# Selective scan at the end of a fused kernel: two replications issued ahead of the restacking, y sums, low part and x's turning moved within the step

## What is computed

```python
xs = stack([x0, x1, x0[..., ::-1], x1[..., ::-1]])     # 4 directions k: rows, columns, both reversed
x_dbl = einsum('bkdl,kcd->bkcl', xs, x_proj_weight)    # -> dts (6), Bs (16), Cs (16)
delta = softplus(einsum('bkrl,kdr->bkdl', dts, dt_projs_weight) + bias)
def step(h, inp):                                      # along the 4096 pixels
    h = exp(d_t[..., None] * A) * h + (d_t * u_t)[..., None] * B_t[:, :, None, :]
    y = einsum('bkdn,bkn->bkd', h, C_t)                # 96 channels x 16 states
ys = ys + Ds * xs; the four directions are turned back and summed; then a norm over channels
```

## Time and profile before

| what | value |
|---|---|
| 3 runs | 5444.3, 5447.71, 5461.19 us; median 5447.71 |
| profiled execution | 5458.66 us, span 5456.5 us |
| busy in the span | PE 4633.9 (85%), DVE 4354.1 (80%), POOL 4137.1 (76%), ACT 3138.7 (58%) |
| first and last scan | start 2764.0 us, end 5366.3 us: 2602.3 us for 128 steps |

### The profile page before, as it was taken

One profiled execution on the slowest core, in us unless ns is written; L12 is line 12 of the kernel. 1 busy time (PEld: TensorE's weight loads), 2 busy tenths in 40 slices (PEclk: granted clock), 3 DMA queues, 4 the chain that ended last, 5 costly groups with the idle time before them and its releaser, 6 DMA issues. The chain is left out here.

```text
span 5456.5 us, 68516 instructions
## 1 busy us (share of the span) xinstructions
PE 4633.9 (85%) x15210; PEld 2099.0 (38%) x15210; DVE 4354.1 (80%) x3524; ACT 3138.7 (58%) x6582; POOL 4137.1 (76%) x1958
## 2 busy tenths in 40 slices
PE   7998887956999999964978888888888888888887
PEld 2332554623666666642522222222222222222222
DVE  4776445452599999997969999999988999999995
ACT  6885555621111111101367788887878778888876
POOL 2454545532589898987869999899998999999993
PEclk9998999977999999977979999999998999999998
DMA  2000101067678787844067777777776777777773
GB/s 52 1 1 15 55 22 51 27 195 203 134 141 151 140 153 140 152 73 99 0 152 186 183 194 183 182 188 177 188 188 170 187 185 187 182 190 179 191 184 98
DMA packets 385380, 733.14 MB, mean 134 GB/s; under 512 B 77948, under 2 KB 119080, under 8 KB 370920
## 3 DMA queue, kind: packets, MB, share of 16 engines
q1 hardware_dynamic: 385128, 730.30, 56.8%
HBM read 594.31 MB, written 82.32 MB: 124 GB/s over the span
## 5 line engine op out<-in xcount | busy, mean ns | idle before, releaser
L2208 POOL TENSOR_TENSOR l_hc<-l_h,l_c_rep 128x1024 f32<-128x1024 f32 x768 | 1805.8, 2364 | 212.3 <-DVE l_h L2279 206.0
L1400 POOL TENSOR_TENSOR l2b_prod<-l2b_v,l2b_attn 128x1568 f32<-128x1568 f32 x276 | 937.9, 3458 | 232.0 <-ACT l2b_attn L1361 117.3
L2279 DVE TENSOR_TENSOR_SCAN l_h<-l_p,l_h,l_bu 128x1024 f32<-128x1024 f32 x448 | 1030.9, 2337 | 71.8 <-ACT l_bu L2116 70.7
L1964 PE MATMUL l_p<-l_stacked,l_pick 96*128 96x512 f32 x1536 | 656.2, 509 | 302.1 <-DVE l_h L2279 301.6
L2263 DVE TENSOR_TENSOR l_bu<-l_du_rep,l_p 128x1024 f32<-128x1024 f32 x512 | 616.5, 1204 | 133.9 <-DMA l_du_rep<-du_scratch 125.1
L1448 DVE TENSOR_REDUCE l2b_osum<-l2b_prod 128x32 f32<-128x1568 f32 x384 | 665.7, 1780 | 63.3 <-POOL l2b_prod L1400 59.5
L2197 POOL TENSOR_TENSOR l_pool_bu<-l_du_rep,l_b_sb 128x1024 f32<-128x1024 f32 x256 | 605.2, 2364 | 40.3 <-DMA l_du_rep<-du_scratch 40.3
L1964 PEld LDWEIGHTS l_p<-l_stacked,l_pick 96*128 96x128 f32 x1536 | 253.1, 196 | 989.2 <-DVE l_h L2279 815.1
L1973 PE MATMUL l_p<-l_hc,l_y_pick 128*32 128x512 f32 x3072 | 582.3, 646 | 3.7 <-POOL l_hc L2208 3.7
L1353 ACT ACTIVATE l2b_logits<-l2b_conv,l2b_this_b 98x512 f32<-98x512 f32 x96 | 66.2, 689 | 861.0 <-PE l2b_conv L1318 861.0
L2279 DVE TENSOR_TENSOR_SCAN l_h<-l_p,l_h,l_pool_bu 128x1024 f32<-128x1024 f32 x224 | 524.7, 2343 | 3.8 <-ACT l_pool_bu L2116 3.5
(11 more groups left out here) (269 smaller groups left out, 9066.2 us busy)
## 6 DMA issues: line engine op xcount, KB each, us to landing
l_du_rep<-du_scratch SPq DMA_DIRECT2D x1536, 256.0 KB, 5.2
l2b_img_high<-qkv_scratch SPq DMA_DIRECT2D x192, 306.2 KB, 5.7
l2b_img_low<-qkv_scratch SPq DMA_DIRECT2D x192, 306.2 KB, 9.5
l_stacked<-l_parts SPq DMA_DIRECT2D x512, 96.0 KB, 2.3
l2b_v<-v_scratch SPq DMA_DIRECT2D x192, 152.0 KB, 6.4
qkv_scratch<-l2a_strip SPq DMA_DIRECT2D x32, 840.0 KB, 5.2
du_scratch<-l_du SPq DMA_DIRECT2D x128, 192.0 KB, 2.1
l_w_raw<-L_w_sed SPq DMA_DIRECT2D x32, 576.0 KB, 3.7
```

The costliest lines, as they stand in the source:

```text
L1400: return eng.tensor_tensor(dst.rearrange("q x (dy dx) -> q x dy dx", dx=WIN), window, attn_half[:, :, unit % 2].rearrange("q x (dy dx) -> ...
L1964: pe.matmul(p_da[p % 2][:, e, :], pick[:, GRP[i] % (Q // DL), :], stacked[:, par, GRP[i] * DL // Q, :], start=True, stop=True).then_inc(s_ ...
L2208: pool.tensor_tensor(hc[:, slot:slot + 2, :], h[:, 2 * p:2 * p + 2, :], c_rep[:, par, :].unsqueeze(1).to_broadcast([128, 2, N]), ALU.mult) ...
L2279: dve.tensor_tensor_scan(flat(h[:, 2 * p:2 * p + 2, :]), flat(p_da[p % 2]), flat(of), state, ALU.mult, ALU.add).then_inc(s_h, 1)
```

## The change

SP issues the first two replications of step n + 1 between `store_du` and `restack`, in the loop and ahead of step 0. PE takes `y_triple` 3 ahead of `replicate(2)`, and `low_mm` ahead of `replicate(3)`. ACT, for k = 0, takes `turn_x` between `take_y` and `low`, and no longer between `b_copy` and `decays(4)`. No instruction is added or taken away.

```diff
                 if more:
                     store_du(n + 1, 1 - par)
+                    for i in range(2):
+                        replicate_du(n + 1, 1 - par, i)
                     sp_.wait_ge(s_rep, G * n)
                     sp_.nop(nofuse=True)
                     restack(n + 1, 1 - par)
-                    for i in range(RING):
+                    for i in range(2, RING):
                         replicate_du(n + 1, 1 - par, i)
...
                 if before:
                     y_triple(n - 1, 2, 1 - par)
+                    y_triple(n - 1, 3, 1 - par)
                 replicate(n, k, 2, par)
                 if before:
-                    y_triple(n - 1, 3, 1 - par)
                     y_whole(n - 1, *before)
+                if n1:
+                    low_mm(n + 1)
                 replicate(n, k, 3, par)
                 if n1:
-                    low_mm(n + 1)
                     b_mm(n + 1, 1 - par, *n1)
...
                 if before:
                     take_y(n - 1, *before)
-                if n1:
-                    low(n + 1)
-                decays(n, k, c, 3)
-                if n1:
-                    b_copy(n + 1, 1 - par)
                 if k == 0:
...
                         turn_x(b, 2 * c)
+                if n1:
+                    low(n + 1)
+                decays(n, k, c, 3)
+                if n1:
+                    b_copy(n + 1, 1 - par)
                 decays(n, k, c, 4)
```

More of the change, by code:

```diff
@@ L1900, in step @@
                     restack(n + 1, 1 - par)
-                    for i in range(RING):
+                    for i in range(2, RING):
                         replicate_du(n + 1, 1 - par, i)
             store_du(0, 0)
+            for i in range(2):
+                replicate_du(0, 0, i)
             restack(0, 0)
-            for i in range(RING):
+            for i in range(2, RING):
                 replicate_du(0, 0, i)
```

## The result

The changed kernel took 5249.23 us (median of 4 runs, 5247.23 to 5254.04); the kernel before, on the same chip, 5454.45 us (4 runs, 5444.3 to 5462.77). The ratio is 0.9626 (95% interval 0.9605 to 0.9647): 205 us are gone where 132 were forecast, and the time lies 13 us under the range.

The account below looks back on a forecast made before the run. DVE was taken to bound the scan, POOL nearly as full. Terms -113 - 20 + 8 - 11 = -136, less 4 for POOL, gave -132: 5316 us against the median 5447.7, range 5262 to 5402.

Parts of the forecast that it names:

- Replications: SP's first two replications ahead of the restacking: nearly all of DVE's 115.3 us wait for them goes, -113 us.
- Rival C: On SP, the replications land no sooner, so the time stays within 0.3% of 5448 us; chance 0.05.
- The copies: Four copies to `l_stacked` on SP start 1.0 us later, still 0.9 us early; some 2 us more before DVE waits; booked 0.
- a wait for `l_stacked` in PE's list: Sign in the changed kernel's profile that the forecast is wrong: PE waiting for the restacked copies; no size given.
- Rival D: Copies to `l_stacked` land so late that `replicate(0)`, `decays(0)` and scan 0 wait every step: slower, say 5490 us; chance 0.05.
- `y_triple` 3 ahead of `replicate(2)`: On PE, `replicate(2)` and `decays(2)` come 0.99 us later, `y_whole` keeps its place: +8 us, bounds 0 and +64.
- `low_mm`: On PE ahead of `replicate(3)`: `low` and `decays(3)` gain 0.36 us in 56 steps of k = 1 and 3, -20 us.
- The 4 us added back for POOL: Correction to the sum from -136 to -132 us, as POOL is nearly full and its waits for scans don't vanish.
- x's turning: On ACT ahead of `low` in k = 0: scan 3 waits 0.65 us, scan 4 nothing; -11 us, bounds -26 and +8.
- The ceiling: The most the change can give is DVE's idle time in the scan, 205.2 us; POOL allows no more than 214.
- rival A: More comes back: PE idles less without DVE's wait ahead of scan 5, lifting TensorE's clock; 5250 to 5286 us; chance 0.13.
- Rival B: Another DVE wait takes the place, scan 5 for its `decays` or scan 2 for its later one; about 5380 us; chance 0.17.

Follow-up runs that it names:

- e9_rep4: The changed kernel with four instead of two replications ahead of the copies to `l_stacked`: 5410.95 us, ratio 0.9944 to the kernel before.
- e10_rep6: The changed kernel with six instead of two replications ahead of the copies to `l_stacked`: 5825.25 us, ratio 1.0703 to the kernel before.
- e6_y3_only: The kernel before with only `y_triple` 3 moved ahead of `replicate(2)` on PE: 5391.78 us, ratio 0.9898.
- e1_rep_only: The kernel before with only SP's order changed, two replications ahead of the restacking: 5335.9 us, ratio 0.9801.
- e2_no_rep: The changed kernel with SP's order put back, replications behind the restacking; PE's and ACT's moves kept: 5355.91 us, ratio 0.9842.

## Why the prediction was too small

**Replications, right.** Booked -113; alone they gave -102, on top of the other edits -107 (5355.91 to 5249.23; 104 of the scan). The first goes out 2.26 us behind the store's issue, where the prediction said 2.4. Rival C, that they land no sooner, is refuted. 11.6 us are left of the wait; in one such step (image 1, k = 0, chunk 6), the only one read, the fourth replication lands 2.6 us behind the third, while the trace shows transfers on two queues of kind "instruction". That these cause it is not shown.

**The copies, right for two ahead, wrong in what they had to spare.** In the step shown the last copy is issued some 1.9 us into its group's 2.46 and lands at 14.08 us of the step. The figure by bytes in order was 3674.9, which is 14.07 of that step.
The prediction named a wait for `l_stacked` in PE's list as a sign of being wrong. There was none before, and 28 stand there now, 21.5 us together. They hardly reach DVE, whose scans wait 7.6 us for ACT in all. PE had less room than the 0.9 us worked out: `replicate(0)` starts at 14.53 of the step now (4800.64), 0.76 sooner than before and not 0.36, and so 0.5 us behind the landing. DVE's room, put at "about 0.9 + 2 us", was some 2 in all: by `e9_rep4` it waits where copies land past 16.0 to 16.5 us of the step, and not only past 16.9. The prediction's own rows give 1.2 to 1.6 us, and not 2, on top of the 0.9 (3679.6 less 1.8 for `decays(0)` and less 0.47 to 0.87 from PE's start to ACT's is 3676.9 to 3677.3, for a `replicate(0)` at 3675.76). Beyond that `e9_rep4` loses 1.3 us a step (162 / 127) and `e10_rep6` 4.5. Rival D's mechanism is real, and two replications stay some 2 us short of it.

**The step that failed: "`y_triple` 3 ahead of `replicate(2)`".** "0 here, and `y_whole` keeps its place" priced one triple as a delay of `replicate(2)` and nothing else, +8. The cost came: scan 2's waits for ACT rose from 3.3 to 11.2 us in `e6_y3_only`. But the order also took 0.23 us from PE's way to `y_whole`, so that `y_whole` did not keep its place; everything behind it, `low` and `decays(3)` too, came sooner. Some 24 us that scan 3 lost in k = 1 and 3 went with it, much of k = 0's waits, and 13 us of the wait for the replication. Alone it is worth -57.

**The same step's neighbour, `low_mm`, mis-sized.** Booked -20 for k = 1 and 3; there scan 3 lost 24 us less (28.7 to 4.9). What was left out is k = 0, where waits for ACT fell by 23 (39.5 to 16.8), k = 2, where 9 us went (8.8 to 0), the wait for the replication, which fell by 15 with the copies ahead of it, and the clock, which fell 25 times for 51. How much of k = 0's share is the order and how much the clock isn't told apart. The k = 1 step of the earlier trace rows was taken for all that the edit touches. Alone it is worth -62. Since both edits remove the same waits, they are not to be added: all three small edits together are worth -82 for the -23 booked, and those 59 us are most of the 73 that the forecast lacked. The 4 us added back for POOL were not needed either: its waits for scans fell from 206.0 to 15.7 us.

**x's turning, right in size, in part by luck.** -11 booked; putting it back costs 12 us of scan and 13 in the medians. But the rows behind the -11 don't show: scan 3 was to wait 0.65 us in each of these steps and waits 1.7 us in all steps of k = 0 together, and what comes back with the turning put back is 4.9 us at scan 4, where 17.4 stood before, and 9 falls of the clock in k = 0 for 2. The turning on its own was not run.

**The ceiling was too low.** 205.2 us of idle time were named as the most that the change can give; scan time fell by 203.0, yet 26 us of waits remain. DVE's busy time fell too, by 23.2 us (2397.1 to 2373.9). The lengths of its instructions, summed over the groups of its lines, fell by only 5.8 (2471.2 to 2465.4); the other 17.4 are overlap. An instruction that needn't wait starts some 0.08 us before the recorded end of the one ahead (4795.69 + 4.58 - 4800.20 = 0.07), and one that waits doesn't. So each wait removed gives back about 0.08 us more than its idle time shows (17.4 us for some 230 waits).

**Rivals.** The time is at the lower edge of rival A's (5250 to 5286), and its condition holds only in part: the number is right by luck. ACT's waits did fall by far more than 31 us and the clock did come back, but not "because" DVE waits less ahead of scan 5: `e1_rep_only` had 51 falls as well, `e2_no_rep` 15. Rival B (scan 2 or scan 5 as the next wait) is refuted: both read `l_pool_bu`, and its waits for L2121 are 1.0 us in all.

## What to carry to other kernels

Price a moved instruction by the place of everything behind it on its engine, in each kind of step that runs it, and not only by what it now stands in front of; a reorder that looks like a delay can shorten the way. When two edits aim at one wait, measure them apart and together, since their gains don't add. Of a transfer that is moved back, work out the room of its first reader and that of the engine that bounds the loop: here they were 0.5 us on PE and some 2 on DVE, and a landing 3 us later cost over three quarters of the gain.

## What was not expected of the hardware

Two groups of y matmuls back to back reach the next group in 1.85 us; with another group between them one takes 0.99 and the detour 0.66 more, and in all 0.23 us is saved by not alternating. The lower clock came in 51 short stretches of 5 us each on average, and a change of order cleared all but 5.
